# Moving a softmax's maxima half a step forward and putting identity products in front of turnings and scores, in the third phase of a four-layer transformer kernel

## The chip, the cores and the metric

The kernel runs on one core of a Trainium2 chip. The metric is the device time of one execution in microseconds. A core has TensorE (PE; its weight loads are listed as PEld), VectorE (DVE), ScalarE (ACT), GpSimd (POOL) and SyncE (SP), which issues most of the DMAs. Each engine runs its own list of instructions in order, and they wait for each other on semaphores. TensorE's clock is granted at one of two levels, 1.2 or 2.4 GHz; a granted clock of 1.00 is 2.4.

## The reference

The input x is 32 batches of 128 rows of 128 numbers. Four layers are added to it one after the other, each a cross-attention over the context (16 heads) and a feed-forward block, both on a layernorm of x:

```
x = x + L0_xattn(norm(x), ctx);  x = x + L0_ffn(norm(x))     # mixture of 8 experts
x = x + L1_xattn(norm(x), ctx);  x = x + L1_ffn(norm(x))     # quantised feed-forward
x = x + L2_xattn(norm(x), ctx);  x = x + L2_ffn(norm(x))     # 64 slots, top 8, a GRU step
x = x + L3_xattn(norm(x), ctx);  x = x + L3_ffn(norm(x))     # mixture of 8 experts, top 2
```

The part that matters here is the attention of layers 2 and 3: scores q k', a softmax over the keys (row maximum, exponential, sum, division), and the product of the weights with the values. Heads have 8 numbers in layer 2 and 64 in layer 3.

## The kernel before

The work on x goes in 8 groups of 4 batches. The third phase (from the call of `next_iteration` at line 1417) does the end of layer 1's feed-forward, all of layer 2 and all of layer 3 in one software pipeline. It is an order written out by hand: every engine runs the same loop over half steps `hs` (`for hs in range(FIRST, LAST + 1)`), and in each half step does its share of the unit that is due, with other work in between (`work(place, hs)`). A **unit** is eight score tiles of 128x128: eight heads of one batch in layer 2, two heads of four batches in layer 3. Tables give each unit its half step: the three first groups of layer 2 take half steps 0 to 23 (`FILL = 3`, `NU = 8`), and from 24 on units of layer 2 and of layer 3 take turns, one unit in each half step. Up to half step 51 the units are `alternating`: their scores go to banks 0 and 1 of PSUM for even units and to two others for odd ones (`score_bank`), and TensorE makes them one half step ahead.

A unit n passes through the engines like this:

- TensorE, half step n-1: `scores(n)` (L1958 for layer 2, L1965 for layer 3; 8 products), after it waited until ScalarE's exponentials have freed the banks.
- VectorE: `maxima(n)` (L2545), one reduce over 128x1024 that writes the eight negated maxima `nm`. For an alternating unit it is the first thing that VectorE does in half step n.
- ScalarE, half step n: eight exponentials (L2166) with their row sums, four and four (the two halves). In between it copies the first half of the unit before out of PSUM (L2174, `p_hi`).
- VectorE: the reciprocals of the sums (`sums_inv`, L2553), the first half's in half step n, the second half's in n+1.
- GpSimd: `norm`, the multiplication with the reciprocals (L2214), which counts up `p_normed`.
- TensorE, half step n+1: turning (transposing) four tiles of each half into bank BANK_T (L2017). The first half waits for `p_lo` of the unit before and for `p_normed`, the second for `p_hi` and `p_normed`. Between the halves stand `values` for the unit before (L1931, L1939), `work(1, hs)` and the scores of the unit that follows.
- ScalarE copies the first half (`p_hi`, L2174), VectorE the second (`p_lo`, L2570).
- TensorE, half step n+2: `values`, into BANK_PV, which ScalarE copies out (L2184, L2191).

TensorE's order in a half step is work(0), first turning, values, work(1), the scores of the next unit, second turning, work(2). VectorE's is: maxima of unit n, reciprocals of unit n-1's second half, work(1), reciprocals of unit n's first half, the copy of unit n-1's second half, work(2). The other work that the prediction names: output rows of layer 2 (L1780), layer 3's projections of queries (L1754), keys (L1761) and values (L1788) and its output (L1770), which share one bank and are copied by ScalarE (L2087) or, the keys, by VectorE (L2343); the masked queries of layer 2 (L2372, VectorE); the slots' steps (L1824 to L1890). Already now `idle_work` (L1737) issues products of the identity with itself before the first units, in half steps -4 to -1, whose results nothing reads.

The core of TensorE's loop and of VectorE's:

```python
                                pe.wait_ge(n2["p_lo"], p)
                            pe.wait_ge(n2["p_normed"], 2 * p + 1 + half)
                            for k in range(4):
                                m = pe.transpose(ps[:, BANK_T, k * S:(k + 1) * S],
                                                 pb[:, p % 2, (4 * half + k) * S:(4 * half + k + 1) * S], ident)
                    if n in alternating:
                        maxima(n)
```

Of the kernel before, what the change touches and what calls it, by code (L numbers as in the profile page):

```python
# [34 lines left out]
P = 128  # L35
# [9 lines left out]
NU = G * H // BLK  # L45
# [65 lines left out]
def build(nc, x_d, ctx_d, ctxT_d, mask0_d, mask1_d, w_d, r_d, rank_d, we0_d, we3_d, big3_d, wg_d, wu_d, wd_d, out_d):  # L111
    with ExitStack() as stack:
        def sb(name, shape, dt=F32):
            return stack.enter_context(nc.sbuf_tensor(name, shape, dt))
# [20 lines left out]
        half = sb("half", [P, G])  # L135
# [42 lines left out]
        ps = stack.enter_context(nc.psum_tensor("ps", [P, 8, 512], F32))  # L178

        def W(name, p=P):  # L180
            a, n = W_AT[name]
            return w[0:p, a:a + n]
# [11 lines left out]
        ident = W("ident")  # L194
# [342 lines left out]
        for key in sorted(tile_table, key=lambda key: (key[1], key[2])):  # L537
            g, kind, t = tile_table[key]
            if kind in ("turn", "hidden"):
# [3 lines left out]
                else:  # L543
                    k = NT0 * g + t
# [875 lines left out]
        FILL = 3  # L1420
# [8 lines left out]
        unit_at = {hs: n for n, (hs, _, _, _) in enumerate(units)}  # L1429
# [27 lines left out]
        BANK_T, BANK_PV, BANK_A, BANK_B, BANK_X, BANK_Z = range(2, 8)  # L1457
# [13 lines left out]
        for g in range(ND):  # L1471
            after = tiles_from[-1] + len(window[-1]) if g else 0
            start = max(MOE_AT[g] + 9, after)
# [17 lines left out]
        for g in range(ND):  # L1491
            in_tail = len(window[g]) == TAIL_WINDOW
            for at, place, kind, i in sorted(TAIL_TABLE if in_tail else TABLE, key=lambda row: row[:3]):
                hs = tiles_from[g] + at
# [18 lines left out]
        alternating = [n for n, unit in enumerate(units) if unit[0] < MOE_FROM]  # L1513

        def score_bank(n):
            return BANK_X if n in alternating and n % 2 else 0

        def score_bank_free(n):
            before = [k for k in range(n) if score_bank(k) == score_bank(n)]
            return before[-1] + 1 if before else 0  # L1520
# [5 lines left out]
        for hs, place, item in order:  # L1526
            g, kind, i = item
            if kind in ("turn", "hidden"):
                bank = TAIL_BANKS[uses % len(TAIL_BANKS)] if hs >= TAIL else BANK_X
# [3 lines left out]
            elif i == 0 or (i >= NSH and (i - NSH) % 4 == 0):  # L1533
                q = quad_of(i)
                bank = BANK_A if hs >= TAIL and (NQ + 1) * g + q & 1 else BANK_Z
# [69 lines left out]
        with nc.Block() as block:  # L1605
# [71 lines left out]
            def _(pe):  # L1677
# [54 lines left out]
                                          start=(c == 0), stop=(c == C3 - 1))  # L1732
                        m.then_inc(moe["expert"], 1)

                def idle_work(count):
                    for k in range(count):
                        pe.matmul(ps[:, BANK_PV, k % 4 * P:(k % 4 + 1) * P], ident, ident, start=True, stop=True)  # L1737

                def work(place, hs):
                    if hs == L2_AT[0][0] - 4 and place == 0:  # L1740
                        idle_work(10)
                    if hs == L2_AT[0][0] - 3 and place == 2:
                        idle_work(14)
# [197 lines left out]
                                                  pt[:, p % 2, k * S:(k + 1) * S], start=True, stop=True)  # L1941
                        m.then_inc(n2["pv"], 1)

                def scores(n):
                    _, layer, g, t = units[n]
                    bank = score_bank(n)
                    if score_bank_free(n):
                        pe.wait_ge(n2["exps"], 2 * score_bank_free(n))
                    if layer == 2:
                        b, c = divmod(t, 2)  # L1950
                        if c == 0:
                            pe.wait_ge(n2["q_ready"], G * g + b + 1)
                            if g:
                                pe.wait_ge(n2["k_col"], g)
                        for k in range(BLK):
                            i, a = divmod(k, 2)
                            at = 32 * (2 * c + a)
                            m = pe.matmul(ps[:, bank + a, i * S:(i + 1) * S], qm[at:at + 32, i, b * S:(b + 1) * S],  # L1958
                                          keys[g % 2][at:at + 32, b * S:(b + 1) * S], start=True, stop=True)
                    else:  # L1960
                        pe.wait_ge(n2["q_col"], IC3 * g + t + 1)
                        pe.wait_ge(n2["k3_col"], IC3 * g + t + 1)
                        for b in range(G):
                            for a in range(2):
                                m = pe.matmul(ps[:, bank + a, b * S:(b + 1) * S],  # L1965
                                              q3[t % 2][64 * a:64 * a + 64, b * S:(b + 1) * S],
                                              k3[t % 2][64 * a:64 * a + 64, b * S:(b + 1) * S], start=True, stop=True)
                    m.then_inc(n2["scores"], 1)
# [34 lines left out]
                for hs in range(FIRST, LAST + 1):  # L2003
                    n, follows = unit_at.get(hs), unit_at.get(hs + 1)
                    if n is not None and n not in alternating:
                        scores(n)
                    work(0, hs)
                    p = unit_at.get(hs - 1)
                    for half in range(2):
                        if p is not None:  # L2010
                            if half:
                                pe.wait_ge(n2["p_hi"], p + 1)
                            elif p:
                                pe.wait_ge(n2["p_lo"], p)
                            pe.wait_ge(n2["p_normed"], 2 * p + 1 + half)
                            for k in range(4):
                                m = pe.transpose(ps[:, BANK_T, k * S:(k + 1) * S],  # L2017
                                                 pb[:, p % 2, (4 * half + k) * S:(4 * half + k + 1) * S], ident)
                            m.then_inc(n2["transposed"], 1)
                        if half == 0:  # L2020
                            values(hs)
                            work(1, hs)
                            if follows in alternating:
                                scores(follows)
                    work(2, hs)
                    if hs == DENSE_AT:
                        for kind, i in DENSE_STEPS:
                            dense(kind, i)
# [242 lines left out]
            def _(v):  # L2271
# [47 lines left out]
                def combine(g):  # L2319
                    x = x_group(g)  # L2320
                    v.wait_ge(moe["gathered"], 16 * 2 * G * (g + 1))
                    v.wait_ge(moe["b2_added"], g + 1)
                    for b in range(G):
                        m = v.scalar_tensor_tensor(x[:, b, :], yg3[:, b, :], sort3[g].gab[:, b:b + 1], x[:, b, :], ALU.mult,
                                                   ALU.add)
                    m.then_inc(moe["first_added"], 1)
                    v.wait_ge(moe["first_added"], g + 1)
                    for b in range(G):
                        m = v.scalar_tensor_tensor(x[:, b, :], yg3[:, G + b, :], sort3[g].gab[:, G + b:G + b + 1],
                                                   x[:, b, :], ALU.mult, ALU.add)  # L2330
                    m.then_inc(moe["combined"], 1)
# [208 lines left out]
                def maxima(n):  # L2540
                    v.wait_ge(n2["scores"], n + 1)
                    if n >= 2:
                        v.wait_ge(n2["exps"], 2 * (n - 1))
                    bank = score_bank(n)
                    v.tensor_reduce(nm[:, n % 2, :], ps[:, bank:bank + 2, :].rearrange("p a (j k) -> p (a j) k", k=S), AX,  # L2545
                                    ALU.max, negate=True).then_inc(n2["maxed"], 1)

                def sums_inv(n, half):
                    at = 8 * (n % 2) + 4 * half
                    v.wait_ge(n2["exps"], 2 * n + half + 1)  # L2550
                    if n >= 2:
                        v.wait_ge(n2["p_normed"], 2 * (n - 2) + half + 1)
                    v.reciprocal(rcs[:, at:at + 4], sums[:, at:at + 4]).then_inc(n2["sums_turned"], 1)  # L2553

                for hs in range(FIRST, LAST + 1):
                    n, p = unit_at.get(hs), unit_at.get(hs - 1)
                    if n in alternating:
                        maxima(n)
                    if p is not None:
                        sums_inv(p, 1)  # L2560
                    if n is not None and n not in alternating:
                        maxima(n)
                    work(1, hs)
                    if n is not None:
                        sums_inv(n, 0)
                    if p is not None:
                        v.wait_ge(n2["transposed"], 2 * p + 2)
                        if p >= 2:
                            v.wait_ge(n2["pv"], p - 1)
                        v.tensor_copy(pt[:, p % 2, 4 * S:8 * S], ps[:, BANK_T, :]).then_inc(n2["p_lo"], 1)  # L2570
                    work(2, hs)
                    if hs == DENSE_AT:
                        for kind, i in DENSE_STEPS:
                            dense(kind, i)
                            if (kind, i) == ("output", COMBINE_AFTER):
                                combine(ND - 1)
# [85 lines left out]
```

## Time and profile before

| | |
|---|---|
| median of 3 runs | 2077.67 us (2077.08 to 2080.63) |
| the profiled execution | 2078.95 us, span of its instructions 2077.2 us |
| busy: TensorE | 1855.0 us (89%), weight loads 1511.7 us |
| VectorE | 1474.6 us (71%) |
| ScalarE | 1303.1 us (63%) |
| GpSimd | 633.4 us (30%) |
| mean granted TensorE clock | 0.965 |

The page also gives the busy share and the clock in 40 slices of the span (52 us each):

```
PE   7998989989999997678889889999999998888879
DVE  7987978878788885767765766767767565655456
PEclk9999999999999998978899999999999999999999
```

A digit is a tenth. The third phase's units begin in slice 17 (878 us). In slices 17 to 20 TensorE's busy digits are 6, 7, 8 and 8 with clock digits 9, 7, 8 and 8. Busy time of TensorE grows when its clock is low, so a share alone does not tell how much work was done. "Idle before" in a row is time in which that engine did nothing before the instruction; what ended the wait stands behind the arrow.

### The profile page before, as it was taken

How to read it: one execution, taken by the hardware profiler on the slowest of the kernel's cores; microseconds unless marked ns; L12 is line 12 of the kernel's file. 1: busy time of each engine (PE TensorE's matmuls, PEld its weight loads, DVE VectorE, ACT ScalarE, POOL GpSimd, SP SyncE). 2: the span in 40 equal slices, each digit the busy share in tenths (PEclk: the TensorE clock that was granted, in tenths of full speed). 3: DMA queues.
4: the chain of work that ended last, by engine and by line, in shares of the span. 5: the costliest groups of instructions: out<-in, count | busy, mean ns of one | idle time of the engine just before them, and what ended most of it. 6: DMA issues, size and time to landing. Idle time of an engine off the chain costs nothing.

```text
span 2077.2 us, 50116 instructions
## 1 busy us (share of the span) xinstructions
PE 1855.0 (89%) x17733; PEld 1511.7 (73%) x17733; DVE 1474.6 (71%) x3843; ACT 1303.1 (63%) x4466; POOL 633.4 (30%) x640
## 2 busy tenths in 40 slices
PE   7998989989999997678889889999999998888879
PEld 6777878778888775566666667787778776667765
DVE  7987978878788885767765766767767565655456
ACT  6876656656667785466677766666666654545432
POOL 2112121423222300133434353353443423333321
PEclk9999999999999998978899999999999999999999
DMA  8013464554553101300000022223312223232351
GB/s 266 17 62 107 135 174 134 149 149 131 153 154 108 29 9 64 103 20 25 26 1 21 2 66 63 80 63 94 95 54 80 67 80 92 85 97 76 103 161 39
DMA packets 129734, 178.45 MB, mean 86 GB/s; under 512 B 10192, under 2 KB 91024, under 8 KB 129232
## 3 DMA queue, kind: packets, MB, share of 16 engines
q1 hardware_dynamic: 121808, 159.51, 25.6%
q0 software_dynamic: 7680, 15.74, 2.4%
q8 instruction: 145, 2.38, 0.5%
q14 instruction: 101, 0.83, 0.1%
HBM read 141.26 MB, written 33.95 MB: 84 GB/s over the span
## 4 chain that ended last, share of the span: by engine, by line
PE 38%; DVE 9%; ACT 5%; issue 4%; POOL 1%; DMA 0%; DVEq 0%; ACTq 0%; SPq 0%
PE ps L1720 5%; PE ps L2017 5%; PE ps L1965 3%; PE ps L1770 3%; PE ps L1958 3%; PE ps L1754 3%; ACT pb L2166 2%; PE ps L1939 2%; PE ps L1761 2%; PE ps L1731 2%; PE ps L1780 2%; DVE nm L2545 1%; PE ps L1788 1%; PE ps L1987 1%; PE ps L1931 1%
## 5 line engine op out<-in xcount | busy, mean ns | idle before, releaser
L2166 ACT ACTIVATE pb<-ps,nm 128x128 f32<-128x128 f32 x1024 | 363.2, 377 | 194.8 <-DVE nm L2545 194.8
L2214 POOL TENSOR_TENSOR pb<-pb,rcs 128x512 f32<-128x512 f32 x256 | 268.7, 1050 | 658.2 <-DVE rcs L2553 657.4
L965 ACT ACTIVATE pb<-pb,nm 128x128 f32<-128x128 f32 x1024 | 312.9, 393 | 34.4 <-DVE nm L1269 32.4
L2570 DVE COPY pt<-ps 128x512 f32<-128x512 f32 x128 | 88.3, 690 | 198.1 <-PE ps L2017 198.0
L2166 ACT ACTIVATION_READ_ACCUMULATOR pb<-ps,nm 128x1 f32 x1024 | 221.8, 217 | 0.0
L2545 DVE TENSOR_REDUCE nm<-ps 128x8 f32<-128x1024 f32 x128 | 156.0, 1219 | 61.0 <-PE ps L1965 38.7
L2017 PE MATMUL ps<-w,pb 128*128 128x128 f32 x1024 | 167.0, 288 | 23.3 <-ACT pt L2174 11.0
L1269 DVE TENSOR_REDUCE nm<-pb 128x8 f32<-128x1024 f32 x128 | 156.2, 1220 | 4.4
L2017 PEld LDWEIGHTS ps<-w,pb 128*128 128x128 f32 x1024 | 121.2, 147 | 47.3 <-ACT pt L2174 20.4
L844 PE MATMUL ps<-w,pb 128*128 128x128 f32 x1024 | 141.6, 280 | 8.3 <-ACT pb L965 8.1
L2174 ACT ACTIVATE pt<-ps 128x512 f32<-128x512 f32 x128 | 76.9, 601 | 93.5 <-PE ps L2017 93.4
L1720 PE MATMUL ps<-hT,big 128*128 128x128 f32 x840 | 117.1, 284 | 14.5 <-DVE hT L2316 13.4
L1720 PEld LDWEIGHTS ps<-hT,big 128*128 128x128 f32 x840 | 105.1, 195 | 34.1 <-DVE hT L2316 21.0
L844 PEld LDWEIGHTS ps<-w,pb 128*128 128x128 f32 x1024 | 119.9, 145 | 13.8 <-issue 11.0
L957 ACT ACTIVATE pt<-ps 128x512 f32<-128x512 f32 x128 | 76.3, 596 | 63.9 <-PE ps L844 62.6
L698 PE MATMUL ps<-h_all,big 128*128 128x128 f32 x736 | 103.6, 286 | 13.4 <-DMA big<-in_we 7.5
L698 PEld LDWEIGHTS ps<-h_all,big 128*128 128x128 f32 x736 | 92.6, 197 | 19.9 <-issue 7.4
L950 ACT ACTIVATE ou<-ps 128x256 f32<-128x256 f32 x128 | 48.4, 378 | 88.2 <-DVE h_all L1251 48.1
L706 PE MATMUL ps<-big,hT 128*128 128x128 f32 x736 | 101.3, 282 | 0.0
L2048 ACT ACTIVATE hT<-ps 128x256 f32<-128x256 f32 x133 | 50.9, 383 | 74.4 <-PE ps L1720 73.8
L706 PEld LDWEIGHTS ps<-big,hT 128*128 128x128 f32 x736 | 91.7, 195 | 6.1 <-issue 2.9
L1754 PE MATMUL ps<-h_all,big 128*128 128x512 f32 x128 | 71.5, 640 | 26.2 <-ACT h_all L2087 26.2
(383 smaller groups left out, 4416.1 us busy)
## 6 DMA issues: line engine op xcount, KB each, us to landing
big<-in_we SPq DMA_DIRECT2D x92, 514.0 KB, 3.7
big<-in_we SPq DMA_DIRECT2D x109, 384.0 KB, 3.0
sorted_out<-big SPq DMA_DIRECT2D x27, 256.0 KB
big<-sorted_in SPq DMA_DIRECT2D x7, 960.0 KB, 5.9
sorted_in<-big SPq DMA_DIRECT2D x4, 1472.0 KB, 12.5
big<-sorted_in SPq DMA_DIRECT2D x20, 256.0 KB, 4.2
hidden<-h_all SPq DMA_DIRECT2D x7, 512.0 KB, 3.0
h_all<-hidden SPq DMA_DIRECT2D x7, 512.0 KB, 3.8
```

The lines of the kernel that those rows point to most:

```text
L698: m = pe.matmul(ps[:, 5, c * P:(c + 1) * P], w1_0[:, k % NWS, c, :], xsT0[:, (NQ0 * g + t // 4) % 4, (t % 4) * P:(t % 4 + 1) * P], start=T ...
L706: m = pe.matmul(ps[:, 7, (t % 4) * D:(t % 4 + 1) * D], hT[:, k % 4, c * P:(c + 1) * P], w2_0[:, k % NWS, c, :], start=(c == 0), stop=(c == ...
L844: m = pe.transpose(ps[:, 2 + k // 4, (k % 4) * S:(k % 4 + 1) * S], pb[:, p % 2, k * S:(k + 1) * S], ident)
L965: m = a.activation(pb[:, n % 2, k * S:(k + 1) * S], pb[:, n % 2, k * S:(k + 1) * S], ACT.Exp, bias=nm[:, n % 2, k:k + 1])
L1269: v.tensor_reduce(nm[:, n % 2, :], buf, AX, ALU.max, negate=True).then_inc(s["maxed"], 1)
L1720: m = pe.matmul(ps[:, bank, (2 * half + c) * P:(2 * half + c + 1) * P], weights[:, half, c, :], rows_T, start=True, stop=True)
L1754: pe.matmul(ps[:, BANK_A, :], q3_w[:, c, :], yT3[g % 2], start=True, stop=True)\
L2017: m = pe.transpose(ps[:, BANK_T, k * S:(k + 1) * S], pb[:, p % 2, (4 * half + k) * S:(4 * half + k + 1) * S], ident)
L2166: m = a.activation(pb[:, n % 2, e * S:(e + 1) * S], ps[:, score_bank(n) + half, k * S:(k + 1) * S], ACT.Exp, bias=nm[:, n % 2, e:e + 1], a ...
L2214: g_.tensor_tensor(p4, p4, r4.unsqueeze(2).to_broadcast([P, 4, S]), ALU.mult).then_inc(n2["p_normed"], 1)
L2545: v.tensor_reduce(nm[:, n % 2, :], ps[:, bank:bank + 2, :].rearrange("p a (j k) -> p (a j) k", k=S), AX, ALU.max, negate=True).then_inc(n2 ...
L2570: v.tensor_copy(pt[:, p % 2, 4 * S:8 * S], ps[:, BANK_T, :]).then_inc(n2["p_lo"], 1)
```

## The change

`idle_work` gets an argument for the bank. In half steps 1 to 25 (`FILLED`) TensorE issues two identity products in front of the scores of the next unit, into the bank that the scores then overwrite, and two in front of each of the two turnings, into the turnings' bank, ahead of the wait for `p_normed`; in half step 1 the first turning has twelve in front instead of two. On VectorE the maxima of an alternating unit are taken in the half step before: behind the reciprocals of the current unit's first half and ahead of the copy of the unit before. This holds for units 0 to 51.

```diff
-                def idle_work(count):
+                def idle_work(count, bank=BANK_PV):
                     for k in range(count):
-                        pe.matmul(ps[:, BANK_PV, k % 4 * P:(k % 4 + 1) * P], ident, ident, start=True, stop=True)
+                        pe.matmul(ps[:, bank, k % 4 * P:(k % 4 + 1) * P], ident, ident, start=True, stop=True)
+
+                FILLED = range(1, NU * FILL + 2)
...
-                def scores(n):
+                def scores(n, hs):
                     _, layer, g, t = units[n]
                     bank = score_bank(n)
                     if score_bank_free(n):
                         pe.wait_ge(n2["exps"], 2 * score_bank_free(n))
+                    if hs in FILLED:
+                        idle_work(2, bank)
...
                                 pe.wait_ge(n2["p_hi"], p + 1)
                             elif p:
                                 pe.wait_ge(n2["p_lo"], p)
+                            if hs in FILLED:
+                                idle_work(12 if hs == 1 and not half else 2, BANK_T)
                             pe.wait_ge(n2["p_normed"], 2 * p + 1 + half)
...
                             if follows in alternating:
-                                scores(follows)
+                                scores(follows, hs)
...
                 for hs in range(FIRST, LAST + 1):
-                    n, p = unit_at.get(hs), unit_at.get(hs - 1)
-                    if n in alternating:
-                        maxima(n)
+                    n, p, follows = unit_at.get(hs), unit_at.get(hs - 1), unit_at.get(hs + 1)
                     if p is not None:
                         sums_inv(p, 1)
...
                     if n is not None:
                         sums_inv(n, 0)
+                    if follows in alternating:
+                        maxima(follows)
                     if p is not None:
                         v.wait_ge(n2["transposed"], 2 * p + 2)
```

## Rows read from the trace of the kernel before

**Rows 1.** Busy time by stretch: from-to, length, busy us (instructions) per engine, clock, DMA.

```profile
878.45:1041.75 163.30, 128.64 (x1206) 98.34 (x1202) 110.93 (x293) 106.71 (x473) 65.90 (x61) 0.81 0.07 23
1041.75:1224.90 183.15, 162.71 (x1581) 125.03 (x1582) 125.97 (x343) 132.05 (x541) 72.55 (x69) 0.99 0.06 19
```

**Rows 2.** The same view, cut to the stretches at 1.2 GHz (order: PE, PEld, DVE, ACT, POOL).

```profile
883.30:903.80 20.50, 16.50 (x122) 13.12 (x122) 9.78 (x22) 11.39 (x59) 7.26 (x7) 0.50 0.11 36
...
910.60:917.40 6.80, 6.80 (x34) 5.51 (x35) 3.68 (x9) 3.80 (x19) 2.08 (x2) 0.51 0.00 0
...
934.50:941.30 6.80, 5.77 (x36) 5.21 (x40) 3.59 (x10) 3.37 (x19) 1.79 (x3) 0.51 0.01 2
...
948.20:951.60 3.40, 3.40 (x17) 2.80 (x16) 2.16 (x5) 2.91 (x14) 3.06 (x3) 0.50 0.04 14
...
958.40:968.60 10.20, 9.29 (x60) 8.11 (x61) 6.95 (x28) 6.40 (x22) 2.08 (x2) 0.50 0.00 1
...
989.10:999.40 10.30, 7.53 (x53) 6.39 (x53) 7.00 (x16) 5.21 (x26) 2.34 (x3) 0.50 0.01 2
...
1016.40:1019.80 3.40, 3.03 (x27) 2.09 (x25) 3.16 (x5) 2.92 (x13) 3.40 (x4) 0.51 0.00 0
```

**Rows 3.** TensorE's waits, 878.45 to 1041.75: us in total, times, longest.

```profile
PE ps L2017 <- POOL pb L2214: 6.3, 3, 3.8
PE ps L2017 <- ACT pt L2174: 3.5, 4, 1.5
PE ps L1958 <- DVE qm L2372: 3.5, 3, 1.3
PE ps L1958 <- ACT pb L2166: 3.4, 4, 2.0
PE ps L2017 <- DVE pt L2570: 3.1, 4, 0.8
PE ps L1867 <- DVE h_all L2469: 2.4, 1, 2.4
PE ps L1958 <- issue: 2.2, 2, 1.1
```

**Rows 4.** ScalarE's wait for the maxima in the same stretch.

```profile
ACT pb L2166 <- DVE nm L2545: 37.2, 22, 3.7
```

**Rows 5.** One half step in order of time: start, us, engine, line.

```profile
939.63 1.21 DVE L2545 TENSOR_REDUCE nm<-ps 128x8 f32<-128x1024 f32 x1
...
941.80 1.16 PE L1958 MATMUL ps<-xm,qm 32*128 32x128 f32 x16
...
942.27 0.61 ACT L2174 ACTIVATE pt<-ps 128x512 f32<-128x512 f32 x1
...
942.93 0.66 PE L2017 MATMUL ps<-w,pb 128*128 128x128 f32 x4
...
943.62 0.69 DVE L2570 COPY pt<-ps 128x512 f32<-128x512 f32 x1 [0.90 <-PE ps L2017]
...
944.56 1.21 DVE L2545 TENSOR_REDUCE nm<-ps 128x8 f32<-128x1024 f32 x1
```

**Rows 6.** Three identity products at 2.4 GHz (L1321) and what follows; ten at 1.2.

```profile
846.85 0.83 PE L1321 MATMUL ps<-w 128*128 128x128 f32 x6
847.52 0.38 PE L1332 MATMUL ps<-pt,wgq 128*128 128x512 bf16 x1
...
861.20 4.61 PE L1737 MATMUL ps<-w 128*128 128x128 f32 x20 [2.66 <-PEq L495]
```

**Rows 7.** The first turning, with the wait before it.

```profile
882.74 0.66 PE L2017 MATMUL ps<-w,pb 128*128 128x128 f32 x4 [3.78 <-POOL pb L2214]
```

**Rows 8.** Units 26 to 51: TensorE's waits for VectorE's key copy, and one such copy.

```profile
PE ps L1780 <- DVE h_all L2343: 3.9, 6, 0.9
PE ps L1770 <- DVE h_all L2343: 2.4, 4, 0.9
...
1041.14 0.69 DVE L2343 COPY h_all<-ps 128x512 f32<-128x512 f32 x1 [0.17 <-PE ps L1761]
```

More of the change, by code:

```diff
@@ L2005, in _ @@
                     if n is not None and n not in alternating:
-                        scores(n)
+                        scores(n, hs)
                     work(0, hs)
```

## The prediction

> **What bounds the kernel now.** I read the table of stretches first, because the page averages phases with different limits. In the filled stretch (unit 0's maxima to unit 25's, 878.45 to 1041.75) TensorE is busy 128.64 of 163.30 us, so it idles 34.7 us, at a mean granted clock of 0.81; the other engines have more room, VectorE 110.93, ScalarE 106.71 [rows 1]. The rest of the units with alternating banks, to unit 52 (1041.75 to 1224.9), runs at clock 0.99 with TensorE busy 162.71 of 183.15 [rows 1]. Next, the same view cut where the clock changes: seven stretches of 1.2 GHz lie in the filled part, 61.4 us long, and TensorE is busy 16.50+6.80+5.77+3.40+9.29+7.53+3.03 = 52.3 us in them [rows 2]. Work that took 52.3 us at 1.2 GHz takes 26.2 at 2.4, so 26 us of TensorE's time here is clock.
>
> Then TensorE's waits. In front of turnings (L2017) and scores (L1958) it idles 6.3+3.5+3.5+3.4+3.1+2.2 = 22.0 us; the other 12.7 lie in front of layernorm, slot and projection steps, the longest 2.4 us on a VectorE result [rows 3]. ScalarE, for its part, waits 37.2 us in 22 pieces for VectorE's maxima [rows 4]. The order of one half step shows why: maxima at 939.63, done 940.84; ScalarE's four exps and then the copy of the first turning at 942.27; second turning 942.93; VectorE's copy of it 943.62; one small VectorE piece, and the next maxima only at 944.56 [rows 5]. Each link waits for the one before, a loop of 4.93 us, though the scores those next maxima read were begun at 941.80 and took 1.16 [rows 5]. So a light step is bound by this loop through three engines, a heavy one by TensorE, and any step at 1.2 GHz by TensorE at half rate.
>
> **The change part by part.** *Maxima moved.* Nothing is added or removed on VectorE; 1.21 us leave the place behind second turning, copy and late work, and stand behind the first half's reciprocal. The loop is cut: scores end at about 942.96, so the maxima could end at 944.2 rather than 945.77, and ScalarE's exps start when ScalarE is free. Queued behind the moved reduce are the copy of the second turning and VectorE's late work. In an unfilled step the second turning ends 0.6 us after the scores and the maxima 1.2 after them, so that copy starts about 0.6 us late; with two identity products in front of the turning (below) it ends 1.1 after the scores, and the copy is late by 0.1 to 0.2. TensorE waits for this copy before its next first turning, usually behind a microsecond or more of projections; in steps without them the delay shows, but the wait on maxima goes at the same time. No DMA and no queue entry moves. Also no wait is new to VectorE except that it now stands for scores a half step sooner; behind it stand that copy and late work.
>
> *Identity products.* Per half step 1 to 25: two in front of each of two turnings and two in front of the scores, with ten more at step 1: 25x6+10 = 160. One product is two instructions. Three products start at 846.85 and what follows them at 847.52: 0.67/3 = 0.223 us each at 2.4 GHz; ten took 4.61 us at 1.2 GHz, so about 0.46 [rows 6]. At full clock they add 160x0.223 = 35.7 us of TensorE; at half clock twice that.
>
> The Trainium skill ("TensorE: Matmul & The Clock Gate", section on the back-to-back issue gap) gives about 81 ns for each load-and-multiply pair of 128 columns. By that figure, as an estimate, the products would cost 160x2x0.081 = 26 us and the sum would come out 10 us lower; the rows show 0.112 us per instruction for this very form, so the measured one stands.
>
> What hides them: the waits behind them. The twelve at step 1 are 2.7 us into a wait of 3.78 for GpSimd's normalising [rows 7]; 1.1 remains. For the other 150 the cover is the remaining 18 us of waits before turnings and scores, which the moved maxima would in any case shrink. Without cover each costs its full 0.22.
>
> *The clock.* Products raise TensorE's load. No row shows this phase filled; the nearest from the two sides are the later units, where TensorE idles 20 of 183 us and has clock 0.99, and the present state, 35 of 163 and 0.81 [rows 1]. Filled, it would idle about 14 of 156, nearer the first, so I take 8 us of 1.2 GHz left of 61.4, which costs 4 us (bounds: 0 and 20 us of cost, the latter with 40 us at half clock).
>
> *Sum for the filled stretch.* TensorE at full clock: 128.6-26.2 = 102.5, plus 35.7 is 138.1. Waits outside the filled places 12.7, less a little since the other engines are now earlier relative to TensorE: 11; the opening wait 1.1; new or left-over waits in front of turnings 2; so 14 (bounds 8 and 21). Half clock 4. Total 156, against 163.3: **7 us less**. Steps at half clock and light steps get shorter; steps in which TensorE is already full at 2.4 GHz get longer, by up to 6x0.223 = 1.3 us.
>
> *Units 26 to 51, maxima alone.* TensorE idles 20.4 us. The moved reduce pushes the copy of layer 3's keys (L2343) behind it: now it starts at 1041.14, just 0.17 after TensorE delivered, and TensorE waits for it 3.9 us in six cases and 2.4 in four [rows 8]. It would start some 0.2 us later, at most 13x0.2 = 2.6 us lost. Against it stand waits on late exps, at most 3 us. I take 0, bounds -3 and +3. Units after 51 and the other phases are unchanged: 0.
>
> The profiled execution took 2078.95 us (span 2077.2, 1.75 around it), 1.28 above the median of the three runs, 2077.67. 2078.95-7.3 = 2071.65; on the median **2070.4 us**.
>
> **The rivals.** *Waits merely move (about even).* Twelve us of waits outside stay, and behind the identity products some 7 of 22 survive because ScalarE or GpSimd set the step: 138.1+19+5 = 162, a gain of 1, with units 26 to 51 even: 2076.5. For it: a heavy step, where TensorE hardly waits, pays all of its 1.3 us (the later units, 89% busy, show such steps [rows 1]). Against: ScalarE's 37 us of waits lose their cause.
>
> *The clock stays low (slower).* Place: half steps 6 to 22. The twelve products remove the first long wait and so the first stretch, but the other six, 40.9 us [rows 2], stay if short products don't prevent them. Then 138.1+14+20.5 = 172.6, 9 us more: 2087. It decides from 22 us of half clock on, since 163.3-138.1-14 = 11.2 us, doubled, is break-even. Against it: the stretches at 910.6 and 948.2 had TensorE busy all through and ended after 6.8 and 3.4 us [rows 2], and in the later units the clock held. The Trainium skill (same page, "Why this matters for your kernels") warns only of long idle gaps between bursts; by that rule the small products would buy nothing but the first stretch, which is this rival. Its section on a second failure mode says that frequent short idling also makes the clock swing. Rows here speak for the second: no wait of TensorE other than the opening one is above 2.4 us [rows 3], and the clock fell six more times.
>
> *More than summed (faster).* Waits outside shrink too, as ScalarE and VectorE run ahead: 138.1+8+1 = 147, and 3 us in the later units: 19 less, 2059.
>
> *The copy behind the moved maxima decides (slower).* If the late copy costs TensorE 0.4 us in each of 51 steps, 20 us, less the 7: 13 more, 2091. The projections between make this unlikely. That the change does nothing is excluded: 320 instructions must run.
>
> **How the numbers follow.** A measurement can tell about 0.2%, 4.2 us, from no change. Forecast (4 to 13 us less) 0.42; more than summed 0.16; about even 0.20; clock stays low, or only part of it returns, 0.16; late copy 0.06. So faster 0.58, same 0.20, slower 0.22. Range 2059 to 2085: it takes in the large gain and the even case, and the milder half of the clock rival.
>
> **What would show it.** Unit 0's to unit 25's maxima take about 156 us; clock there above 0.95; TensorE's busy time about 142; ScalarE's wait on maxima from 37 below 12 us; waits at turnings and scores from 22 below 5; units 26 to 51 within 3 us of 183. The sum is wrong if the clock stays under 0.9, or if idle at full clock stays above 21 us; the view of the moved maxima is wrong if TensorE's waits on the copy at L2570 grow.

## The result, and the profile after

The changed kernel took 2090.49 us (median; 2088.91 to 2095.76), the kernel before beside it 2077.67. The ratio on record is 1.0051 with a 95% interval of 1.0026 to 1.0076 (the two medians alone would give 1.0062): **slower**, where 2070.4 and faster had been forecast. A second, later comparison (e9 below) gave 1.0029 (1.0007 to 1.0052).

The profiled execution of the changed kernel took 2092.47 us, its span is 2090.7 (before 2077.2). Where the 13.5 us lie is seen best when both kernels are cut at the same work, the start of TensorE's scores of units 0, 26 and 52. Busy time by stretch, the kernel before (from-to, length, busy us and instructions of PE, PEld, DVE, ACT, POOL, clock, DMA):

```profile
877.24:1045.21 167.97, 133.07 (x1264) 102.24 (x1264) 114.03 (x301) 110.13 (x482) 66.94 (x62) 0.82 0.07 22
1045.21:1223.70 178.49, 158.28 (x1533) 121.27 (x1529) 123.31 (x337) 128.03 (x532) 70.31 (x67) 0.99 0.06 20
1223.70:2077.20 853.50, 782.42 (x6672) 624.88 (x6671) 532.53 (x1502) 473.77 (x1760) 301.67 (x294) 0.99 0.27 82
```

The same for the changed kernel; the first two rows answer to [rows 1], whose cuts at the maxima don't suit here because the maxima themselves have moved:

```profile
877.28:1049.64 172.36, 156.09 (x1580) 126.62 (x1581) 115.29 (x304) 112.01 (x488) 66.37 (x63) 0.96 0.07 22
1049.64:1233.61 183.97, 162.03 (x1533) 124.79 (x1532) 120.23 (x332) 126.84 (x526) 69.16 (x67) 0.97 0.06 19
1233.61:2090.70 857.09, 786.01 (x6672) 627.14 (x6671) 532.54 (x1502) 473.95 (x1760) 301.70 (x294) 0.99 0.27 82
```

So 4.4 us were lost in the filled stretch, 5.5 in units 26 to 51 and 3.6 behind them; up to unit 0 the two agree within 0.1 us. In the filled stretch the clock did come back, 0.82 to 0.96, and TensorE's idle time halved, 34.9 to 16.3 us. Its busy time rose all the same.

Below, half clock stands for 1.2 GHz. Three numbers make each stretch comparable: the **idle** time (length less busy), the **clock's cost** (half of what TensorE is busy in stretches at 1.2 GHz) and the rest, the **work** at full clock. For the filled stretch:

```
                 length   work   clock's cost   idle
before           168.0    106.8      26.3       34.9
changed          172.4    149.7       6.4       16.3
difference        +4.4    +42.9     -19.9      -18.6
```

The waits in it (878 to 1042), changed kernel, which answer to [rows 3] and [rows 4]:

```profile
PE ps L1737 <- DVE pt L2576: 4.6, 7, 0.8
PE ps L1869 <- DVE h_all L2475: 2.5, 1, 2.5
PE ps L1962 <- DVE qm L2378: 1.5, 2, 1.0
...
PE ps L2023 <- POOL pb L2220: 0.8, 1, 0.8
...
DVE nm L2551 <- PE ps L1962: 38.1, 21, 4.9
...
ACT pt L2180 <- PE ps L2023: 18.9, 20, 2.8
ACT pb L2172 <- DVE nm L2551: 14.9, 10, 3.4
```

ScalarE's wait for the maxima fell from 37.2 to 14.9 us, but its wait for the turnings rose to 18.9 (7.0 before). VectorE waits as long as before, now for the scores (38.1 us) where it had waited for the turnings:

```profile
DVE pt L2570 <- PE ps L2017: 38.0, 21, 3.2
```

The 22 us of waits of TensorE in front of turnings and scores are 7. And most light half steps, those with little other work between their two turnings, take exactly 5.36 us, which a loop of two engines, VectorE and TensorE, makes. In order of time, changed kernel, from one maxima to the next (compare [rows 5]):

```profile
921.51 1.23 DVE L2551 TENSOR_REDUCE nm<-ps 128x8 f32<-128x1024 f32 x1 [2.26 <-PE ps L1962]
...
922.65 0.68 DVE L2576 COPY pt<-ps 128x512 f32<-128x512 f32 x1
...
923.39 0.71 PE L1737 MATMUL ps<-w 128*128 128x128 f32 x4
...
923.94 0.60 PE L2023 MATMUL ps<-w,pb 128*128 128x128 f32 x4
...
924.47 0.62 PE L1933 MATMUL ps<-pt,va 128*8 128x128 f32 x16
...
925.02 0.71 PE L1737 MATMUL ps<-w 128*128 128x128 f32 x4
...
925.66 1.16 PE L1962 MATMUL ps<-xm,qm 32*128 32x128 f32 x16
...
926.87 1.23 DVE L2551 TENSOR_REDUCE nm<-ps 128x8 f32<-128x1024 f32 x1 [2.38 <-PE ps L1962]
```

Maxima, copy, two products, first turning, values, two products, scores, maxima. The old loop of 4.93 us through ScalarE is gone; four of the six products stand in the new one.

### The profile page after: what moved, and what is told of

The parts are those of the page before. It is cut to its first block, busy times and chain, and to the rows that moved or that the text cites. A ratio compares the mean times of both kernels' runs of the same rounds, so it can differ in the third digit from the quotient of the medians.

```text
span 2090.7 us, 50704 instructions
## 1 busy us (share of the span) xinstructions
PE 1887.1 (90%) x18053; PEld 1543.4 (74%) x18053; DVE 1473.1 (70%) x3843; ACT 1304.1 (62%) x4466; POOL 631.8 (30%) x640
## 4 chain that ended last, share of the span: by engine, by line
PE 40%; DVE 8%; ACT 5%; issue 5%; POOL 1%; DMA 0%; DVEq 0%; ACTq 0%; SPq 0%
PE ps L1720 5%; PE ps L2023 4%; PE ps L1772 3%; PE ps L1962 3%; PE ps L1969 3%; PE ps L1756 3%; PE ps L1941 2%; PE ps L1737 2%; ACT pb L2172 2%; PE ps L1731 2%; PE ps L1763 2%; PE ps L1790 2%; PE ps L1782 1%; PE ps L1991 1%; PE ps L1933 1%
## 5 line engine op out<-in xcount | busy, mean ns | idle before, releaser
L2023 PE MATMUL ps<-w,pb 128*128 128x128 f32 x1024 | 159.8, 279 | 9.3 <-ACT pt L2180 5.9
L844 PE MATMUL ps<-w,pb 128*128 128x128 f32 x1024 | 141.6, 280 | 8.3 <-ACT pb L965 8.0
L2023 PEld LDWEIGHTS ps<-w,pb 128*128 128x128 f32 x1024 | 119.3, 143 | 23.4 <-ACT pt L2180 13.5
```

The source lines that it names most:

```text
L844: m = pe.transpose(ps[:, 2 + k // 4, (k % 4) * S:(k % 4 + 1) * S], pb[:, p % 2, k * S:(k + 1) * S], ident)
L2023: m = pe.transpose(ps[:, BANK_T, k * S:(k + 1) * S], pb[:, p % 2, (4 * half + k) * S:(4 * half + k + 1) * S], ident)
```

## The experiments

The theory after the result was A: a product costs more than priced (42.9/158 = 0.27 us instead of 0.223; the last two of the 160 stand behind the scores of unit 26, outside the stretch) and lies in TensorE's path; the clock and the moved maxima help. The rival was B: the maxima in front of the copy are what slowed the kernel. The diffs are against the changed kernel. `moved(m)` says for which units the maxima are taken half a step early; for the others `maxima(n)` stands where it stood. "Stretch" is from the scores of unit 0 to those of unit 26.

**e1: the maxima alone.**

```diff
-                FILLED = range(1, NU * FILL + 2)
+                FILLED = ()
```

> All units of alternating banks have their maxima moved, no identity products. Stretch from the scores of unit 0 to those of unit 26: before 168.0 us with 61.5 us at 1.2 GHz and 34.9 idle, with the whole change 172.4 us with 13.6 and 16.3. Theory A (the price of the products was too low and lies in TensorE's path; the moved maxima help): about 160 us here, half clock still 40 to 60 us, units 26 to 52 within 4 us of before (178.5), whole kernel 3 to 9 us faster than before. Theory B (the maxima in front of the copy are what slowed it): stretch at 168 or more and units 26 to 52 4 us or more longer, whole kernel 4 us or more slower.

**e2: the products alone** (`moved` is never true).

> All 160 identity products, maxima where they were. Theory A: half clock in the stretch to unit 26 falls to 5 to 20 us, products at 0.27 us each in TensorE's path and those ahead of the second turning inside the old loop; the stretch comes to 172 to 178 us, units 26 to 52 unchanged (178.5 within 1 us but for the clock), whole kernel 5 to 10 us slower. Theory B: without the maxima in front of the copy the products are nearly free, the stretch is at 165 or less, whole kernel faster.

**e3: only the twelve products of the opening**, maxima as before.

```diff
-                FILLED = range(1, NU * FILL + 2)
+                FILLED = (1,)
...
-                    if hs in FILLED:
-                        idle_work(2, bank)
...
-                            if hs in FILLED:
+                            if hs in FILLED and not half:
```

> Only the twelve products ahead of the first turning of half step 1, in a wait of 3.8 us; everything else as before. If that wait is what brings the first 20 us of half clock: steps 2 to 5 shorten by 4 to 8 us in sum and the whole kernel is 4 to 8 us faster. If the clock falls at the next short waits all the same: half clock within 10 us of before, kernel within 2 us of before.

**e4: all products, maxima moved for units 0 to 25** (`moved(m)` is `m <= 25`).

> The whole change, but the maxima moved for units 0 to 25 alone. If the loss after unit 26 (5.5 us in the profile) is the moved maxima's, by later copies of keys: units 26 to 52 at 178.5 us again and the whole kernel about 2082 to 2084, some 6 to 8 us faster than with the whole change. If that loss was chance of the clock, the whole kernel stays at about 2088 to 2090.

Measured, ratio to before with its interval, and from the profile the stretch with its three parts, then units 26 to 52:

```
            ratio (95%)                stretch  work   clock  idle   26 to 52  (1.2 GHz in it)
e1 maxima   1.0013 (0.9991 to 1.0034)   165.2   105.8   28.8  30.6    187.2      17.1
e2 products 1.0052 (1.0024 to 1.0080)   173.5   150.9    1.7  20.9    182.1      10.2
e3 opening  0.9995 (0.9976 to 1.0015)   164.8   110.0   22.5  32.4    180.0       6.8
e4 to 25    1.0011 (0.9988 to 1.0035)   172.3   149.7    6.4  16.3    180.7       6.8
```

B falls for the stretch: the products alone are as slow as the whole change, with 44 us more work at full clock than before, 24.6 less clock and 14.0 less idle (the profile is of the fastest of e2's eight executions, so its clock may be a lucky draw; the work is not). A holds in sign: the maxima alone shorten the stretch, though by 2.8 us and not by 8. The whole kernel of e1, forecast 3 to 9 us faster, can't be told from before, and its units 26 to 52 took 187.2 us where 178.5 within 4 had been expected. Without products the loop is 4.23 us long, as these rows of e1 show:

```profile
920.86 1.23 DVE L2551 TENSOR_REDUCE nm<-ps 128x8 f32<-128x1024 f32 x1 [0.68 <-PE ps L1962]
...
922.00 0.68 DVE L2576 COPY pt<-ps 128x512 f32<-128x512 f32 x1
...
922.74 0.66 PE L2023 MATMUL ps<-w,pb 128*128 128x128 f32 x4
...
923.33 0.62 PE L1933 MATMUL ps<-pt,va 128*8 128x128 f32 x16
...
923.88 1.16 PE L1962 MATMUL ps<-xm,qm 32*128 32x128 f32 x16
...
925.09 1.23 DVE L2551 TENSOR_REDUCE nm<-ps 128x8 f32<-128x1024 f32 x1 [1.25 <-PE ps L1962]
```

From 4.23 to 5.36 are 1.13 us for four products, 0.28 each. But e1's clock is as low as before (64.9 us of 1.2 GHz in the stretch), and gives part of it back. In e3 the twelve products cut the idle time of step 1 from 5.1 to 2.2 us, yet 1.2 GHz begins again in step 2: 51 us of it instead of 61. The expectation that the first 20 us hang on that wait was wrong; and the stretch gained 3.2 us. So this run met its other branch: half clock 10 us less than before, the whole kernel as before. In e4 the idle time of units 26 to 52 is that of before again, 20.3 us. Their code is the same in e2, e3, e4 and before, and their lengths still differ by 3.6 us, with their half clock.

**e5: products and moved maxima in steps 1 to 16 alone** (`FILLED = range(1, 17)`, `m <= 16`).

> Products in half steps 1 to 16 alone, maxima moved for units 0 to 16 alone: the part of the stretch in which the whole change gained. Theory D (a product costs 0.27 us of TensorE's path and pays only where it buys back half clock): scores of unit 0 to unit 17 at 104.6 us as with the whole change (before 108.6), 17 to 26 back at 59.4 with 10 to 14 us of half clock, so 164 in sum (whole change 172.4, before 168.0); whole kernel 1 to 5 us faster than before. If instead the products of half steps 17 to 25 hold the clock of what follows, 17 to 26 shows over 20 us of half clock and over 63 us.

**e6: products ahead of the second turning alone**, and the opening's.

```diff
-                    if hs in FILLED:
-                        idle_work(2, bank)
...
-                            if hs in FILLED:
+                            if hs in FILLED and (half or hs == 1):
```

> Products only ahead of the second turning (two, and the twelve at the opening), maxima moved for units 0 to 25. These two stand beside the maxima and not in the loop maxima, copy, first turning, values, scores, maxima, which took 4.23 us without products and 5.36 with all. Theory D: light steps at 4.3 us at full clock, steps in which TensorE is full 0.55 us longer than without; half clock between 14 and 50 us; stretch to unit 26 at 162 to 167 us. Rival (any product costs the same wherever it stands): light steps at 4.8 us.

**e7: one product in place of two at each place.**

> One product in place of two at each of the three places, twelve at the opening, maxima moved for units 0 to 25. If a product costs 0.27 us: steps 22 to 25 are 0.8 us longer than without (1.6 with two each), light steps 4.8 us; half clock 14 to 30 us; stretch to unit 26 at 164 to 169 us. If the cost is rather one of each place (the change between products and turnings), steps 22 to 25 are over 1.1 us longer.

**e8: the first turning's products ahead of the wait for the copy.**

```diff
+                            if hs in FILLED and p and not half:
+                                pe.wait_ge(n2["exps"], 2 * score_bank_free(follows))
+                                idle_work(2, score_bank(follows))
                             if half:
                                 pe.wait_ge(n2["p_hi"], p + 1)
...
-                            if hs in FILLED:
+                            if hs in FILLED and (half or hs == 1):
```

> All products as in the change, but those of the first turning stand ahead of the wait for VectorE's copy and write to the banks of the next scores; maxima moved for units 0 to 25. Theory of the loop (maxima, copy, first turning, values, scores): light steps fall from 5.36 to 4.8 us, steps in which TensorE is full stay as with the whole change (1.6 longer than before), stretch to unit 26 at 168 to 171 us instead of 172.4. If TensorE's sheer load sets the step and not the loop, light steps stay at 5.36.

```
            ratio (95%)                stretch  work   clock  idle   light steps
e5 1 to 16  0.9987 (0.9965 to 1.0010)   166.5   135.7    8.3  22.5    5.36
e6 second   0.9992 (0.9965 to 1.0019)   166.4   121.4   21.4  23.6    4.22 to 4.31
e7 one each 0.9995 (0.9970 to 1.0020)   169.3   132.7   15.9  20.7    4.91
e8 ahead    0.9997 (0.9970 to 1.0024)   177.3   148.0   14.5  14.8    4.87 to 5.15
```

e5's steps 17 to 25 took 61.8 us with 13.7 of half clock, between the two cases; its stretch gained 1.5 us where 4 had been expected. e6 settles where a product is free: beside the maxima, in light steps, which stay at 4.22 to 4.31 us where e1's loop took 4.23. In full steps, in which TensorE hardly waits, its two products cost 0.49 us. The rival there (4.8 us) falls. In e8 two light steps fell to 4.87 as the loop says, with 0.40 us of waiting for the copy. Two others stopped at 5.14 with TensorE never idle: its own load is then the bound. The other three (5.05 to 5.15) wait 0.40 us for the copy too, and 0.1 to 0.2 for the masked queries. Its stretch missed the expectation (168 to 171) by 6 us, all of it clock: 30.7 us at 1.2 GHz against 13.7. The whole kernels of e5 to e8 can't be told from before.

e7's stretch is just above what was expected (164 to 169), with 33 us of half clock where 14 to 30 had been. It gives the price, with **e15, four products at each place** (run later):

> Four products in place of two at each of the three places (twelve at the opening), maxima moved for units 0 to 25. Steps 23 to 25 took 6.43, 6.53 and 6.72 us without, 0.94 more with one each, 1.6 more with two each. If a place costs 0.10 us and a product 0.22: 2.9 us more than without. If a product costs 0.27 whatever: 3.2 us more. Half clock near 0 in the stretch but for the slot steps.

Step 24 (scores of unit 24 to those of 25) is at full clock in all and TensorE idles only 0.25 us in it:

```
products at each of 3 places:   0      1      2      4        2, at the second turning alone
step 24, us:                   6.53   7.48   8.15   9.49      7.02
more than without:              -     0.95   1.62   2.96      0.49
```

From one to two it is 0.67 and from two to four 1.34 us, so 0.223 for each product, exactly the price that the prediction took. But the first costs 0.317: **a place costs 0.094 us beside its products**, on the mean of the three. The rows show where. Two turnings of one heavy step before:

```profile
1030.89 0.60 PE L2017 MATMUL ps<-w,pb 128*128 128x128 f32 x4
1031.42 0.62 PE L1931 MATMUL ps<-pt,va 128*8 128x128 f32 x16
1031.97 1.16 PE L1958 MATMUL ps<-xm,qm 32*128 32x128 f32 x16
1033.06 0.66 PE L2017 MATMUL ps<-w,pb 128*128 128x128 f32 x4
1033.56 1.06 PE L1788 MATMUL ps<-big,mask1i 128*128 128x128 f32 x8
```

and of the same step in the changed kernel:

```profile
1030.98 0.61 PE L1737 MATMUL ps<-w 128*128 128x128 f32 x4
1031.42 0.60 PE L2023 MATMUL ps<-w,pb 128*128 128x128 f32 x4
1031.95 0.62 PE L1933 MATMUL ps<-pt,va 128*8 128x128 f32 x16
1032.51 0.71 PE L1737 MATMUL ps<-w 128*128 128x128 f32 x4
1033.15 1.16 PE L1962 MATMUL ps<-xm,qm 32*128 32x128 f32 x16
1034.24 0.71 PE L1737 MATMUL ps<-w 128*128 128x128 f32 x4
1034.79 0.60 PE L2023 MATMUL ps<-w,pb 128*128 128x128 f32 x4
1035.22 0.94 PE L1790 MATMUL ps<-big,mask1i 128*128 128x128 f32 x7
```

From products to what follows are 0.44 us at the first turning (the bare price of two), 0.64 ahead of the scores and 0.55 ahead of the second turning. What starts behind `values` and behind the scores starts as late as before (0.56 and 1.09 us; before 0.55 and 1.09), and the second turning, now behind products, leads to the next work after 0.43 us instead of 0.50. So the three places are unequal: the first turning's costs nothing, the scores' about 0.20 us and the second turning's about 0.05, as e6's 0.49 for two products there also says.

What makes the 0.20 and 0.11 no run separates. The Trainium skill ("TensorE: Matmul & The Clock Gate", Part 3) says that a weight load overlaps a running product only where its row group differs. The trace agrees in the pace: the scores' 16 instructions, in tiles of 32 rows that alternate between two row groups, take 1.09 us, 0.07 each, and the identity products, on all 128 rows, 0.11 each. It does not explain the 0.20, for in the kernel before the scores stood behind `values`, which also fills 128 rows. The same page's figure of 81 ns for a pair ("Back-to-back issue gap"), weighed in the prediction, lies under the 0.112 us per instruction that e7 and e15 confirm.

**e9: the whole change again. e10: the opening's products and maxima moved for units 0 to 25**, a version made of the two parts that had helped.

> The whole change once more, beside the others on one chip. Stretch to unit 26 at 172.4 us with 13.7 us of half clock again (it came out the same to 0.1 us in two profiles); units 26 to 52 at 179 us plus half of whatever half clock falls there. Ratio to before 1.002 to 1.007; if it is 1.000, the slowing first measured was mostly chance of the clock.

> Twelve products at the opening alone, maxima moved for units 0 to 25. Each of the two parts shortened the stretch by about 3 us (168.0 to 164.8 and 165.2). If they add: 161 to 163 us, with 45 to 60 us of half clock; kernel 3 to 7 us faster than before. If the half clock comes back elsewhere: 165 us, kernel as before.

**e11: as e10, with eight products ahead of each of two long waits; e12: as e11, with two more ahead of the second turning in steps 2 to 12.**

```diff
+                        if g == 0:
+                            pe.wait_ge(n2["p_lo"], unit_at[hs - 1])
+                            idle_work(8, BANK_T)
                         pe.wait_ge(slot["hid"], g + 1)      # and the same ahead of slot["new"]
```

> As the kernel above, and eight products (1.8 us) ahead of each of two waits of over 2 us in the slot steps 13 and 17, into the turnings' bank. If half clock is bought back cheapest in long waits: nothing added to TensorE's path beyond 0.3 us, half clock 5 to 20 us less than in the kernel above, stretch 156 to 161 us. If short waits bring the clock down all the same: half clock and stretch within 2 us of the kernel above.

> As the kernel above, and two products ahead of the second turning in half steps 2 to 12, where they stand beside the maxima. They cost nothing in light steps and 0.54 us in full ones (five or six of the eleven, 3 us), and hold more of the clock: half clock 10 to 30 us, stretch 155 to 161 us. If they cost more than they hold, the stretch is longer than in the kernel above.

**e13, e14: the kernel before, profiled twice more. e16: e10 again.**

> The kernel before, profiled again. If half clock in a given stretch is chance to a few microseconds, the stretch to unit 26 comes out within 4 us of 168.0 with 50 to 70 us of half clock, and units 26 to 52 at 176.8 plus half of their half clock (3 to 17 us).

> The same once more: how far two profiles of one kernel lie apart in the stretch to unit 26. Over 3 us apart, single profiles tell no difference of 3 us between kernels, and only the times or sums at full clock do.

> The fastest version so far once more: twelve products at the opening, maxima moved for units 0 to 25. Ratio to before 0.993 to 0.998 again if it is real (10 us is more than its stretch shows, 6 us); 1.000 within its interval if the first was chance.

```
            ratio (95%)                stretch  work   clock  idle   26 to 52  (1.2 GHz in it)
e9 whole    1.0029 (1.0007 to 1.0052)   176.5   149.2   11.0  16.3    183.9      10.2
e10         0.9951 (0.9931 to 0.9971)   162.2   109.1   25.9  27.2    183.1      13.7
e16 = e10   0.9964 (0.9950 to 0.9978)   161.7   109.0   25.4  27.3    183.1      13.7
e11         0.9958 (0.9938 to 0.9978)   162.4   113.9   21.5  27.0    181.0       6.8
e12         0.9965 (0.9942 to 0.9989)   162.7   119.7   18.4  24.6    181.0       6.8
e13 before  one time, 2076.3            168.1   106.8   26.4  34.9    178.5       3.4
e14 before  one time, 2084.5            168.7   106.6   28.0  34.1    183.2      13.7
```

Five things follow. First, e10 beats the kernel before twice, medians 2075.18 and 2074.01 us beside 2085.04 and 2082.22 on the same chips, and the changed kernel, 2090.57 beside it in e9's comparison. The two gains of 3 us add: its stretch is 6 us shorter, with 7.7 us less idle time and 2.3 more work. The medians are 10 and 8 us apart; the profiles don't show where the other 2 to 4 lie. Here is the row of e10, with 0.82 of the clock, as low as before:

```profile
873.22:1035.43 162.21, 134.98 (x1290) 104.81 (x1289) 113.53 (x301) 110.23 (x484) 64.98 (x62) 0.82 0.07 23
```

Second, e11 and e12 bought 10 and 17 us of half clock back and won nothing: the work they added (4.8 and 10.6 us) is what they got. Expected had been 156 to 161. Step by step, e11's eight products did pay where they stand: steps 13 and 14 took 12.3 us against 14.2 in e10, steps 17 and 18 12.0 against 15.3. But the steps between, 15 and 16, took 22.3 against 16.5: in both e11 and e12 one stretch of 17.1 us at 1.2 GHz covers them (step 15 alone 15.2 us, 11.4 of it half clock, against 12.0 in e10). What is bought back at one wait came back at another; whether the products brought it there no run tells.

Third, e9 missed: I had taken 172.4 us for firm since two profiles agreed, and the third is 4.1 longer. Its work and idle time are the same to 0.5 us (149.2 and 16.3); the clock alone differs, 23.9 us at 1.2 GHz instead of 13.7.

Fourth, the kernel before shows the same in units 26 to 52, which e14's rows hold (first its stretch, then those units):

```profile
876.07:1044.77 168.70, 134.64 (x1266) 103.00 (x1265) 113.96 (x301) 109.94 (x482) 67.03 (x62) 0.81 0.07 22
1044.77:1227.93 183.16, 162.94 (x1532) 125.24 (x1528) 122.84 (x337) 128.27 (x532) 70.40 (x67) 0.96 0.06 19
```

One kernel, 178.5 or 183.2 us in these units, with 20.2 us idle both times. In the filled stretch the same three profiles agree within 0.7 us, so the 6 us of e10 there, seen twice, stand clear of this chance better than the single 3 us of e1 and e3.

Fifth, e15's work is 182.1 us, its clock nearly whole (6.8 us at 1.2 GHz), its stretch 199.0: doubling the products bought back little that the first dose had not, at 32 us more work.

## Why the prediction was wrong

The profiled execution was to become 7.3 us shorter and its span became 13.5 longer: 20.8 us apart, 11.7 of them in the filled stretch, 5.5 in units 26 to 51 and 3.6 behind them. *What failed* is the sum for the filled stretch: it was to become 7.3 us shorter and became 4.4 longer. Term by term:

- **The price of the products, 160x0.223 = 35.7 us: measured 42.9 (for 158 of them).** This is the step that turned the stretch's sign, 7.2 of the 11.7 us. The marginal price was right (e7 and e15 give 0.223). The row it came from, three products at one place and what followed them at once, has no sign of what a place costs here: 158x0.223 are 35.2 us and 74 places at the mean of 0.094 are 7.0, together 42.2. Products were inserted two by two, so that many changes to and from other work were bought, above all the one between products and scores, and these the prediction did not count.
- The clock, 4 us of cost left: measured 6.4 in the profile (e4 the same, e9 11.0, e2 1.7), some 2.4 of the 11.7. Taken from the nearest rows, it was about right: half clock fell from 61.4 to 13.7 us.
- Idle time, 14 us: measured 16.3, some 2.1 of the 11.7 (the two cuts of the stretch differ by 0.2). Right in kind: the waits in front of turnings and scores mostly went. Step 17 still waits 2.5 us for the slots' VectorE result, and the half clock behind it (10.2 us) stayed.

"Without cover each costs its full 0.22" was thus low, and the cover itself was thin: all three places are in TensorE's path once the step is full, and two of three stand in the new loop in light ones. The sentence on the copy queued behind the moved maxima had the loop in it, but the prediction priced it as a delay of 0.1 to 0.2 us and did not close it: copy, turning, values, scores, maxima. In the unfilled form it takes 4.23 us, so it matters only because products were put inside.

*Units 26 to 51*, forecast 0 within 3: measured +5.5. Of that, idle time is 1.7 (21.9, against 20.2 to 20.9 in all kernels whose maxima stayed there), and it sits where the prediction put it, in TensorE's wait for the key copy, for which the changed kernel's rows answer to [rows 8]:

```profile
PE ps L1782 <- DVE h_all L2349: 6.6, 6, 2.0
...
PE ps L1772 <- DVE h_all L2349: 3.0, 5, 1.2
```

3.9 and 2.4 us before, so 3.3 us more, less what went elsewhere. e1 has 22.4 us idle, the same cost. The forecast had read the copy in [rows 8] as starting 0.17 us after TensorE delivered; the 0.17 is VectorE's own idle time, which the delivery ended, so the copy started at once and had no delay yet. Another 0.3 us is work, the last two products. The other 3.5 us are half clock, 10.2 us against 3.4; e14 reaches 13.7 without any change, so this part is not shown to be the change's. The same holds for the 3.6 us behind unit 52 (same instructions, same idle time, 17.1 us of half clock against 10.2 from unit 100 on; 10.2 in e9). What the change itself costs is then, as an estimate, 4.4 + 1.7 = 6 us, 0.3%. That is e9's ratio too, but the 4.4 holds a clock cost that came out 4.6 us higher in e9's profile, so the agreement is partly luck.

*Rivals.* "The clock stays low" and "the late copy decides" are both wrong, though their times, 2087 and 2091, lie next to the measured one; that is chance. The clock came back, and the wait on that copy grew only from 3.1 to 4.6 us. (The first one's 20.5 us also takes half of the 40.9 us of length; half of the 35.8 that TensorE is busy in them is 17.9.) "Waits merely move" is nearest (162 us), and is short by the same missing term. The slower side had a chance of 0.22 and no rival with this price; the bounds for a product (0.223 hot, 0.46 cold) were taken for its whole cost.

*Signs named beforehand.* The maxima of unit 0 to those of unit 25 in about 156 us: 164.0, though both now stand half a step early. Clock above 0.95: yes, 0.96. ScalarE's wait under 12: 14.9. Waits at turnings and scores under 5: 7. Units 26 to 51 within 3 us: 5.5. Idle time not above 21: 16.3. TensorE's wait on the copy not to grow: it grew by 1.5 us, so this sign against the moved maxima came, weakly. TensorE busy about 142, which was 13 more than before: in the stretch from scores to scores it is 23 more (133.1 to 156.1), and this was the sign that told.

## What to carry to other kernels

Work inserted to keep TensorE's clock up must be charged in full against the path, not against the idle sum, and with it the changes of tile that each place adds: here 160 products bought 20 us of clock and 19 of waiting and cost 43. Of the places tried only one paid clearly, the twelve in the long wait at the opening, about 3 us of the stretch. Beside another engine's work in the loop (e6's place) two products cost nothing in light steps, but neither e6 nor e12 came out faster for them; eight in front of two later long waits (e11) won 5 us there and lost 6 between them. When an instruction is moved in an in-order queue, write down the whole new loop that runs through what is now behind it. And compare stretches by work, clock and idle time apart, since half clock of chance alone moved equal code by up to 5 us.

## What the runs showed of the hardware

- TensorE at full clock took 0.223 us for a further identity product (fp32, 128x128, two instructions), the same from one to two and from two to four at a place, but 0.20 us extra between products and the scores of 32-row tiles, 0.05 net ahead of the second turning (0.49 us for two in e6) and nothing ahead of the first.
- Where 1.2 GHz falls is not fixed by the code. Units 26 to 52 of the unchanged kernel had 3.4, 3.4 and 13.7 us of it in three profiles, and the code ahead of unit 0, which no experiment touches, ended between 872.7 and 881.6 us with 64.9 to 92.2 us at 1.2 GHz.
- A filled opening did not hold the clock: in e3 it fell in step 2, in the changed kernel, with TensorE idle at most 0.85 us of each light step of 5.36, it held from step 1 to step 13. In e11 and e12 eight products in front of each of two long waits kept it up around those waits, and it fell for 17.1 us between them.
